# Attention of an MLA layer on eight cores: the query buffers doubled, the value buffers halved

## What is computed

```python
xn = _layernorm(x)
q_c  = _rms_norm(xn @ wq_down.T, q_norm_w)        # rank 1536
q    = concat(q_c @ wq_up.T, rope(q_c @ wq_rope.T))
kv_c = _rms_norm(xn @ wkv_down.T, kv_norm_w)      # rank 512
k, v = split(kv_c @ wkv_up.T); k = concat(k, rope(xn @ wk_rope.T))
scores = einsum('bqhd,bkhd->bhqk', q, k) * scale  # scale = 1/sqrt(192), causal
out = einsum('bhqk,bkhd->bqhd', softmax(scores), v) @ wo.T
g = silu(ffn(xn))                                 # silu(gate) * up, then down
return x + out * g
```

## Time and profile before

| | us |
|---|---|
| median of the 2 runs shown | 8202.82 |
| the two runs | 8080.14, 8325.51 |
| the profiled execution, its own time | 8082.0 |
| its span on the slowest core, core 7 | 8080.5 |
| spans of the eight cores | 8039.5 to 8080.5 |
| busy in the span: PE 5018.1, DVE 3198.9, ACT 1100.1 | 62%, 40%, 14% |

### The profile page before, as it was taken

The page is one execution under the profiler, slowest core; times in us unless marked ns, Lnnn a source line. Parts: engine busy times, 40 slices in busy tenths (PEclk is TensorE's granted clock), DMA queues, the critical chain, the costliest instruction groups (busy, mean ns, idle before and its releaser), DMA issues.

```text
span 8080.5 us, 69559 instructions; the slowest of 8 cores (8039.5 to 8080.5 us)
## 1 busy us (share of the span) xinstructions
PE 5018.1 (62%) x23736; PEld 2314.3 (29%) x23736; DVE 3198.9 (40%) x7402; ACT 1100.1 (14%) x1169; POOL 275.8 (3%) x220
## 2 busy tenths in 40 slices
PE   3344343247763455555555555555589999899998
PEld 1111111212221122222222222232334444344444
DVE  3445444515556555555555555555210101110111
ACT  1110111200001111111111111212001110011100
POOL 0000000000000000000000000000001110011100
PEclk9677666568885566666666666666699999899999
DMA  4111213550001122121211222211337778977887
GB/s 92 57 52 54 56 47 97 132 95 31 30 28 42 52 60 60 48 62 51 69 52 42 76 57 55 59 49 49 81 115 82 74 78 120 144 73 76 77 121 110
DMA packets 1126584, 567.29 MB, mean 70 GB/s; under 512 B 902240, under 2 KB 1074400, under 8 KB 1117920
## 3 DMA queue, kind: packets, MB, share of 16 engines
q0 software_dynamic: 556416, 169.36, 20.1%
q1 hardware_dynamic: 331744, 280.16, 12.0%
q10 hardware_dynamic: 238080, 113.33, 5.3%
HBM read 618.82 MB, written 113.25 MB: 91 GB/s over the span
## 4 chain that ended last, share of the span: by engine, by line
PE 49%; DVE 25%; issue 8%; ACT 7%; DMA 4%; ACTq 3%; another core or an unknown queue 3%; DVEq 1%; POOL 0%; SPq 0%; POOLq 0%
PE c_psd L1281 8%; PE c_psg L1263 7%; PE c_psu L1268 7%; PE b_pspv L1003 6%; DVE b_srow L1026 5%; ACT b_pb L1094 5%; PE b_pspt L989 5%; DVE b_ptb L1068 4%; ACTq L580 3%; PE b_pswo L1147 3%; DVE b_pb L1058 3%; DVE b_srow L1035 2%; PE a2b_psmm L768 2%; PE a2b_psmm L777 2%
## 5 line engine op out<-in xcount | busy, mean ns | idle before, releaser
L989 PE MATMUL b_pspt<-i,b_pb 128*128 128x128 bf16 x4608 | 575.1, 296 | 899.4 <-DVE b_pb L1058 795.3
L1026 DVE TENSOR_SCALAR_CACHE_REDUCE b_srow<-b_pss 128x512 f32<-128x512 f32 x1152 | 736.9, 688 | 539.0 <-ACT b_pb L1094 472.6
L1094 ACT ACTIVATE b_pb<-b_srow,b_bias 128x512 bf16<-128x512 f32 (+7 forms) x256 | 563.8, 2203 | 2644.1 <-PE b_pss L962 1576.6
L955 PE MATMUL b_pss<-b_kb,b_qng 128*128 128x512 bf16 x1152 | 452.9, 484 | 563.0 <-DVE b_srow L1026 533.4
L989 PEld LDWEIGHTS b_pspt<-i,b_pb 128*128 128x128 bf16 x4608 | 405.0, 128 | 1082.8 <-issue 1061.3
L1281 PE MATMUL c_psd<-c_hdn,c_dw 128*128 128x512 bf16 x2816 | 660.0, 399 | 24.0 <-DMA c_dw<-downT 19.3
L1263 PE MATMUL c_psg<-c_xn,c_gw 128*128 128x512 bf16 x2816 | 640.0, 380 | 41.8 <-DMA c_uw<-upT 41.7
L1268 PE MATMUL c_psu<-c_xn,c_uw 128*128 128x512 bf16 x2816 | 636.5, 379 | 0.0
L1068 DVE COPY b_ptb<-b_pspt 128x512 bf16<-128x512 bf16 x1152 | 484.5, 424 | 368.9 <-PE b_pspt L989 365.6
L1304 DVE TENSOR_TENSOR c_hdn<-c_sg,c_su 128x512 bf16<-128x512 f32 x176 | 121.8, 692 | 1142.1 <-ACT c_su L1342 1142.1
L1003 PE MATMUL b_pspv<-b_ptb,b_vb 128*128 128x256 bf16 x2304 | 469.0, 390 | 100.6 <-DVE b_ptb L1068 100.6
(11 more groups left out here) (124 smaller groups left out, 4694.8 us busy)
## 6 DMA issues: line engine op xcount, KB each, us to landing
c_gw<-gateT POOLq DMA_DIRECT2D x88, 512.0 KB, 6.7
c_uw<-upT POOLq DMA_DIRECT2D x88, 512.0 KB, 8.7
c_dw<-downT POOLq DMA_DIRECT2D x32, 1408.0 KB, 19.5
a_xbuf<-xb SPq DMA_DIRECT2D x32, 1024.0 KB, 4.9
kscr<-a_kst ACTq DMA_DIRECT2D x128, 128.0 KB, 1.9
vscr<-a_vst ACTq DMA_DIRECT2D x512, 32.0 KB, 1.6
a_xbuf<-x_own SPq DMA_DIRECT2D x16, 1024.0 KB, 6.3
xfscr<-a_xfstg ACTq DMA_DIRECT2D x64, 256.0 KB, 4.2
```

The source lines that it names most:

```text
L955: e.matmul(ps_s[s_ * 2 + hh][:], qn_t, kbuf[hp % 2][hh][:, kv_c], start=True, stop=False, skip_group_check=True)
L989: mm_ = e.transpose(ps_pt[bq % 2][:, u * 128:(u + 1) * 128], pb[combo][:, kc * 128:(kc + 1) * 128], i16[:])
L1026: kb.inc(e.tensor_scalar(srow[combo][:, c * 512:(c + 1) * 512], ps_s[combo][:], SCALE, None, ALU.mult, ALU.max, accum_out=mxb[combo][:, c: ...
L1094: kb.inc(e.activation(pb[combo][:, 0:nc_ * 512], srow[combo][:, 0:nc_ * 512], AF.Exp, bias=bias[combo][:], scale=1.0, accum_out=ell[combo] ...
```

## The change

The queries get a second buffer, and their load for group gi waits for the last S of group gi - 2 where it waited for that of gi - 1. The values lose their second buffer, and their load for step g waits for PV of step g - 1 where it waited for that of g - 2. PE takes its operands from the buffers so named. The order of all instructions on all engines stays.

```diff
-            qng = [sb("b_qng0", [128, NH * 256], BF16)]
-            qpg = [sb("b_qpg0", [128, (NH // 2) * 256], BF16)]
+            qng = [sb(f"b_qng{i}", [128, NH * 256], BF16) for i in range(2)]
+            qpg = [sb(f"b_qpg{i}", [128, (NH // 2) * 256], BF16) for i in range(2)]
-            vbuf = [[sb(f"b_vb{i}_{h}", [128, S], BF16) for h in range(2)] for i in range(2)]
+            vbuf = [[sb(f"b_vb0_{h}", [128, S], BF16) for h in range(2)]]
...
                 for gi in range(8):
-                    kb.wgm(e, "p", f"b_smmd_{(gi - 1) * 8 + 7}_1")
+                    kb.wgm(e, "p", f"b_smmd_{(gi - 2) * 8 + 7}_1")
                     kb.inc(e.dma_start(
-                        out=r3(qng[0][:], NH),
+                        out=r3(qng[gi % 2][:], NH),
...
                     kb.inc(e.dma_start(
-                        out=r3(qpg[0][:], NH // 2),
+                        out=r3(qpg[gi % 2][:], NH // 2),
...
-                            sv_ = f"v{hp % 2}{hh}"
-                            kb.wgm(e, "p", f"b_pv_{gih - 2}_{hh}")
+                            sv_ = f"v0{hh}"
+                            kb.wgm(e, "p", f"b_pv_{gih - 1}_{hh}")
                             kb.inc(e.dma_start(
-                                out=r3(vbuf[hp % 2][hh][:, 0:nc_ * 4 * 128], nc_ * 4),
+                                out=r3(vbuf[0][hh][:, 0:nc_ * 4 * 128], nc_ * 4),
...
-                            kb.wgm(e, f"v{hp % 2}{hh}", f"b_v_{gih}_{hh}")
+                            kb.wgm(e, f"v0{hh}", f"b_v_{gih}_{hh}")
...
-                                               vbuf[hp % 2][hh][:, kc * 128:(kc + 1) * 128],
+                                               vbuf[0][hh][:, kc * 128:(kc + 1) * 128],
```

More of the change, by code:

```diff
@@ L948, in emit_s @@
                                     kb.wgm(e, "v", prev)
-                            qe = qpg[0]
+                            qe = qpg[gi % 2]
                             base = hp * 256 + s_ * 128
@@ L953, in emit_s @@
                                 h = 2 * hp + hh
-                                qn_t = qng[0][:, h * 256 + s_ * 128:h * 256 + (s_ + 1) * 128]
+                                qn_t = qng[gi % 2][:, h * 256 + s_ * 128:h * 256 + (s_ + 1) * 128]
                                 e.matmul(ps_s[s_ * 2 + hh][:], qn_t,
```

## The result

The changed kernel is slower: the ratio of its time to that of the kernel before is 1.0166, with a 95% interval of 1.0087 to 1.0245. That is +134 us on 8080, with the interval from +70 to +198. The profiled execution took 8202.15 us against 8082.0; the slowest spans are 8200.6 and 8080.5 us.

A forecast was written before the change was run, and what follows sets the result against it. It took waits between engines to bound the attention phase. Low clock 141 + 83 = 224 us, full clock 63 + 73 = 136, weighed 8 to 2: 206 us on 8082.0, 8288 us; range 8190 to 8430.

The forecast's parts named there:

- The direction and the mechanism: In the attention phase, key and query loads held behind the value load's wait start at T; kernel slower.
- T: Moment in a step when DVE begins L1075 for PV_1; SP's burst of loads was to start there.
- signs named in advance: Profile after: some 60 `b_kb` waits, S wait gone, query load within 1 us of T, A within 1 us.
- A: Last key load's landing after T: 3.4 to 13.2 us with 1 to 8 chunks, mean 16.7 at new groups.
- A + 3.9 - E3: A step's delay: DVE reaching combo 3 after T, less E3, when exponentials end (T + 4.5 to 15.9 us).
- the low-clock figure: PE at 0.50 clock after the wait: 141 us late keys plus 83 us new groups, 224 us, weighted 8 to 2.
- 0.5 us more for the first half of chunk 1: PE does this inside the idle time today, late after the change; step delay A + 4.4 - E3 above 1 chunk.
- The full-clock sum: PE at full clock behind the wait: 63 us for late keys plus 73 us for new groups, 136 us.
- (a): Rival: loads faster when PE and DVE stand still, exponentials cover most; 8198 us, +1.4%, chance 0.18.
- (b): Rival: not slower, S in one stretch raises PE's clock, 56 us back if keys covered everywhere; 8026 us, chance 0.03.
- (c): Rival: keys and values hold each other up, transfers collide with ACT's store; each A 1.5 us longer, 8381 us, chance 0.10.
- (d): Rival: no effect, as SP had passed these waits anyway; 8082 us, chance 0.03.

The follow-up runs named there:

- Experiments 1 to 3: Changed kernel with one query buffer, phase 3395 us; with keys ahead of values on SP, 3262 us; with both, 3261 us.
- Experiment 5: Kernel before with unread matmuls added in PE's idle time: phase 3252, 3235 (11 times nc_), 3224 us (13 times nc_); changed kernel likewise, 3404 us.
- experiment 3: Changed kernel with keys ahead of values on SP and one query buffer: phase 3261 us, 8070.65 us in one run.
- experiment 4: Kernel before, both value buffers, key loads of step g also waiting for PV_1 of step g - 2: phase 3311 us, +53.

## Why the prediction was right or wrong

*The direction and the mechanism: right.* The keys are held behind the value load's wait, the query load comes later and not earlier, both start at T, PE waits for them in 62 steps. Experiments 1 to 3 show that it is the order on SP and nothing of the buffers themselves. These signs named in advance came: 63 waits for `b_kb`, the wait for S gone, the query load within 1 us of T, PE's waits of 12 to 20 us at a new group, 2.4 to 3.1 us more per step with 1 to 4 chunks. Two did not: with 6 to 8 chunks the steps were to lengthen by 1 to 2 us and changed by +0.2, -0.4 and -2.2, and A at a new group was off by 1.4 us, where 1 us was named as the limit.

*The size: too large.* Forecast 206 us, measured 134 by the phase and by the ratio, which is 1.66% and not 2.5%. The forecast time, 8288 us, is 86 us over the profiled execution's 8202. The prediction gave "slower by more than 2%" 0.70 of the chance; the measured ratio lies below that, with 2% still inside its interval.

*The landings: right up to 6 chunks, too late beyond.* A from today's bursts, forecast 3.4 to 13.2, came within 0.3 us up to 6 chunks. At 7 and 8 chunks it was 0.8 and 0.9 too high, and for the new groups 1.4. Of the 196 us that A + 3.9 - E3 was to cost in all 62 steps, 178 came.

*The term that failed: "the low-clock figure is nearer, so I weigh them 8 to 2".* It held for the first groups of S behind the wait, where the clock is 0.50 and combo 3 comes at A + 3.9. It was then carried over to all that follows. The step claimed 0.5 us more for the first half of chunk 1, 28 us in all. Part of this came: with 4 to 8 chunks DVE takes combo 0 of chunk 1 0.7 to 1.0 us behind combo 3, and took it 0.62 behind before. But the step also took the rest of S as unchanged, and there waits went away that had been there, so that the stretch as a whole became 0.5 to 1.2 us shorter per step with 2 chunks or more, 42 us in all. With 4 chunks, DVE's first wait behind combo 3 in the kernel before and in the changed one:

```profile
3405.03 0.69 DVE L1026 TENSOR_SCALAR_CACHE_REDUCE b_srow<-b_pss 128x512 f32<-128x512 f32 x1 [0.61 <-PE b_pss L962]
```

```profile
3482.54 0.69 DVE L1026 TENSOR_SCALAR_CACHE_REDUCE b_srow<-b_pss 128x512 f32<-128x512 f32 x1 [0.40 <-PE b_pss L962]
```

Before, a wait of 0.20 us follows in chunk 2; after, none follows. On average over the steps with 4 chunks combo 2 of chunk 1 came 1.31 us behind combo 1 and comes 0.66 behind it now, as PE does these matmuls in 0.6 us a pair where it took 1.0. The reason is in the windows: before, S is in pieces with idle time between (11.65 us behind chunk 0 with 8 chunks, then 2.14 us within chunk 1), and behind it the clock is low; after, chunk 0 and chunk 1 run in one stretch behind the wait, and the clock is up at 0.90 and 0.95 (4 and 8 chunks) for the rest where it was 0.75 and 0.79. Experiment 5 shows that it is the clock and not the order, least surely with 7 chunks. The rows gave the idle time and the low clock behind it, but the question to ask was what the clock does when the pieces join, and not only what it is after the wait. The sum, 196 + 28 at low clock, should have been 178 - 42: of the 90 us between its 224 and the measured 134, 70 are this term and 18 the landings.

*The full-clock sum, 136 us, is near the result by luck.* It took 1 to 1.5 us off a step on the ground that PE was at full clock right behind the wait, where it is at 0.50, and left the rest of S alone, which is what became shorter; and its landings were 18 us too late.

*Rivals.* (a), faster loads, is out: A is as read. (b) was right in kind and nearly in size (56 us against 42), and was bound to a condition, keys covered everywhere, that it doesn't need. (c) is out, since no A was more than 0.3 us above the forecast, and (d), since PE waits for keys in 62 steps.

## What to carry to other kernels

A wait on a queue that issues in order belongs to all that stands behind it: before a buffer is halved or doubled, list which later loads its wait will hold, and put the loads that are needed first ahead of it. A second buffer brings nothing if its load stands behind another wait that ends later, as the queries' did, and nothing either where no engine waited for that load (experiment 3). When a delay looks cheap because something else covers it, find what the cover is; here it was a store's wait on ScalarE that itself cost 515 us, and the same change would have cost 647 us once that was mended.

## What the runs showed of the hardware

A late load can make the work behind it faster. With 5 chunks and keys just covered (experiment 4), the rest of S became 0.6 us shorter on average, since PE's work on S lay in one stretch; in the step shown it ran at a granted clock of 0.95 instead of 0.82. Useless matmuls in the idle time bring the same (experiment 5: 34 us off the phase at best), but not surely if idle time is left between them and the real work, or within it. With 11 times nc_ matmuls and 8 chunks the clock was at 0.98 from T to combo 3 and yet 0.79 in the stretch after it. With 13 times nc_ they ended 0.2 us ahead of chunk 1 on core 0, PE stood 2.8 us behind its first half, and the clock of the rest was 0.94 in one step and 0.78 in the next.
